# Attention with a transposed score maximum and rescaling on ScalarE, and a convolution over 500 tiles of one bin each, in a graph network kernel

## What is computed

```
feat_all = einsum('ni,rhid->rnhd', inputs, conv_weights)      # 8 relations, 4 heads, 64
el = sum(feat_all[type, src] * attn_l[type], -1)
er = sum(feat_all[type, dst] * attn_r[type], -1)
e  = leaky_relu(el + er, 0.2);  m = segment_max(e, dst)
ex = exp(e - m[dst]);  alpha = ex / segment_sum(ex, dst)[dst]
h  = segment_sum(alpha[..., None] * feat_src, dst) + h_bias
```

```
filt = silu(edge_attr @ Wf1 + bf1) @ Wf2 + bf2                # 20 -> 256 -> 256
agg  = segment_sum(x[dst] * filt, src)
h    = silu(agg @ Wu1 + bu1) @ Wu2 + bu2;  x + batch_norm(h)
```

## Time and profile before

| | us |
|---|---|
| median of 3 runs (lowest, highest) | 4170.91 (4170.29, 4171.05) |
| the profiled execution | 4176.44 |
| its span, first to last instruction | 4174.7 |
| PE busy | 2928.3 |
| DVE busy | 2177.3 |
| ACT busy | 1210.5 |
| POOL busy | 2277.2 |
| mean granted clock of PE | 0.858 of full |

### The profile page before, as it was taken

One profiled execution on the slowest core, in us unless ns is written; L12 is line 12 of the kernel. 1 busy time (PEld: TensorE's weight loads), 2 busy tenths in 40 slices (PEclk: granted clock), 3 DMA queues, 4 the chain that ended last, 5 costly groups with the idle time before them and its releaser, 6 DMA issues. The chain is left out here.

```text
span 4174.7 us, 73619 instructions
## 1 busy us (share of the span) xinstructions
PE 2928.3 (70%) x20296; PEld 2364.7 (57%) x20297; DVE 2177.3 (52%) x5961; ACT 1210.5 (29%) x3266; POOL 2277.2 (55%) x2336
## 2 busy tenths in 40 slices
PE   5199101777777777776379679999999864299990
PEld 1188101555555555555255358888888633288990
DVE  8411002877777777777743557777777444011112
ACT  1123000444444444444223223333333231022220
POOL 2777775777777777777240056666666200511115
PEclk8599655998998999999679789999999875599995
DMA  3344101222222222225100143333335501155533
GB/s 105 108 135 137 40 2 32 63 65 63 63 64 63 64 64 63 64 64 62 23 19 1 47 136 89 90 89 90 90 90 84 52 0 39 49 175 173 171 104 114
DMA packets 209214, 317.71 MB, mean 76 GB/s; under 512 B 63367, under 2 KB 150063, under 8 KB 208388
## 3 DMA queue, kind: packets, MB, share of 16 engines
q0 software_dynamic: 95008, 179.89, 19.9%
q1 hardware_dynamic: 103204, 127.24, 9.4%
q10 hardware_dynamic: 10944, 9.97, 0.7%
HBM read 248.03 MB, written 68.84 MB: 76 GB/s over the span
## 5 line engine op out<-in xcount | busy, mean ns | idle before, releaser
L1402 POOL DMA_INDIRECT conv_got<-xtab,conv_rowidx x588 | 565.8, 962 | 313.2 <-DVE conv_msg L1507 156.6
L806 POOL DMA_INDIRECT att_got<-feat,att_rowidx x588 | 573.2, 975 | 201.5 <-issue 150.2
L294 POOL DMA_INDIRECT table<-l0a_rec,l0a_addr x469 | 458.2, 977 | 216.7 <-issue 146.1
L1454 PE MATMUL conv_pf<-conv_wf,conv_act 128*128 128x256 f32 x2352 | 534.0, 380 | 0.2 <-DVE conv_filt L1502 0.2
L812 POOL DMA_INDIRECT table<-recs_rec,recs_addr x432 | 423.2, 980 | 131.6 <-issue 130.4
L1454 PEld LDWEIGHTS conv_pf<-conv_wf,conv_act 128*128 128x128 f32 x2352 | 447.6, 190 | 76.9 <-issue 0.8
L982 PE MATMUL att_pmax<-all_identb,att_away 128*128 128x512 bf16 x588 | 261.1, 444 | 203.9 <-DVE att_elo L901 203.2
L863 DVE TENSOR_REDUCE att_tmax<-att_pmax 128x4 f32<-128x512 f32 x588 | 373.8, 680 | 31.1 <-PE att_pmax L986 27.6
L986 PE MATMUL att_pmax<-all_identb,att_ehi 128*128 128x128 bf16 x2352 | 383.6, 242 | 0.0
L986 PE MATMUL att_pmax<-all_identb,att_elo 128*128 128x128 bf16 x2352 | 383.3, 242 | 0.0
L1420 ACT ACTIVATE conv_act<-conv_p,conv_bf 128x512 f32<-128x512 f32 x294 | 186.2, 684 | 552.1 <-PE conv_p L1446 552.1
(11 more groups left out here) (336 smaller groups left out, 5074.0 us busy)
## 6 DMA issues: line engine op xcount, KB each, us to landing
moe_w<-in_L_ffn_w SPq DMA_DIRECT2D x96, 512.0 KB
feat<-proj_out SPq DMA_DIRECT2D x30, 1040.0 KB
results<-moe_y ACTq DMA_DIRECT2D x76, 128.0 KB, 1.7
att_got<-feat,att_rowidx POOLq DMA_INDIRECT x588
conv_got<-xtab,conv_rowidx POOLq DMA_INDIRECT x588, 2.8
xtab<-ln_row SPq DMA_DIRECT2D x60, 128.0 KB, 1.7
table<-l0a_rec,l0a_addr POOLq DMA_INDIRECT x469
table<-recs_rec,recs_addr POOLq DMA_INDIRECT x469, 2.1
```

The source lines that it names most:

```text
L294: self.nc.gpsimd.indirect_dma_start(out=self.table, out_offset=bass.IndirectOffsetOnAxis(ap=self.addrs[:, j:j + 1], axis=0), in_=self.recs ...
L806: nc.gpsimd.indirect_dma_start(out=got[g % 3][:, k, :], out_offset=None, in_=feat, in_offset=bass.IndirectOffsetOnAxis(ap=rowidx[:, g * K ...
L1402: nc.gpsimd.indirect_dma_start(out=got[g % 3][:, k, :], out_offset=None, in_=xtab, in_offset=bass.IndirectOffsetOnAxis(ap=rowidx[:, g * K ...
L1454: ins = nc.tensor.matmul(pf[b][:, k, :], act1[s3][:, h, (2 * b + k) * P:(2 * b + k + 1) * P], wf2[:, h, :], start=(h == 0), stop=(h == 1))
```

## The change

In the attention: (1) the pipeline gets a fifth step, with four buffers instead of three for most tiles; the products and sums of a group move from step 2 to step 3, the addition into `acc` from step 3 to step 4. (2) The two bf16 parts of the 16 scores are written into a 128 x 4 x 32 tile `spread` that is otherwise zero; PE turns it (four transposes), ACT copies the result to SBUF (`eT`, 32 x 512), and each tile's maxima matrix is one 512-column matmul for `away` and one 512-column matmul with 32 rows for the scores, in place of 1 + 8 matmuls. (3) The four maxima become one `tensor_reduce` over four PSUM banks, 2048 elements. (4) `acc * keep` is done by ACT, four instructions into `shrunk`; DVE adds the sums with one 260-wide instruction. (5) The type masks are built once for all tiles ahead of the loop. (6) DVE's and ACT's orders in a step are new; bin numbers are read right behind long operations. (7) POOL sends 214 columns of table1 here instead of 432; the rest goes beside the join (12), layer norm 1 (26), the first routing (24), the first mixture (167 instead of 37) and layer norm 2 (26).

In the convolution: table1 has 500 tiles, each of one bin (the ranking pads a bin to 128 edges, not to 512), so 125 groups of 4 tiles whose bins may differ; the sums of the four tiles stay apart, two to a PSUM bank, and DVE makes four additions per group, each with its own bin. The three PSUM banks of the sums are now used two per group.

The diff, cut to its core:

```diff
-ET = 588 (both tables)
+ET1 = 500 (table1)
-COLS1 = ROUND * (ET // K - 3), EJ - ROUND * (ET // K - 3)
+COLS1 = ET // K - 4 + (ET // K - 4) // 2, 12, 26, 24, 167, 26
...
@@ attend, gpsimd
-                if g >= SLOTS:
-                    pool.wait_ge(f_ready, g - 2)
-                    pool.wait_ge(last_ready, (g - 2) * LAST)
+                if g >= SLOTS:
+                    pool.wait_ge(f_ready, g - SLOTS + 1)
+                    pool.wait_ge(last_ready, (g - SLOTS + 1) * LAST)
...
-                for i in range(max(g - SLOTS, 0) * ROUND, max(g - SLOTS + 1, 0) * ROUND):
+            sends = [0 if g < SLOTS else 1 + g % 2 for g in range(GROUPS)]
+                for i in range(sum(sends[:g]), sum(sends[:g + 1])):
...
@@ attend, vector, one step, new order
+                if 0 in parts:
+                    wait_positive(dve, sum_ready, t - 3)
+                    wait_positive(dve, away_ready, t - 3)
+                    v.tensor_tensor(oh[u] ...).then_inc(oh_ready, 1)
+                if 2 in parts:
+                    bin2 = bin_of(dve, t - 2)
+                if 3 in parts:
+                    dve.wait_ge(ex_ready, g + 1)
+                    wait_positive(dve, sum_ready, g - 1)
+                    v.tensor_tensor(f[(u - 3) % 2] ...).then_inc(f_ready, 1)
+                if 4 in parts:
+                    bin4 = bin_of(dve, t - 4)
+                if 1 in parts:
+                    (er picked, reduced, z, e, the two parts into spread).then_inc(e_ready, 1)
+                if 2 in parts:
+                    dve.wait_ge(max_ready, g + 1)
+                    v.tensor_reduce(tmax[:, :], pmax[:, :, :, :].rearrange("p k h e -> p h k e"), AX.XY, ALU.max)
+                    (mnew, drop, mparts[0], m, mparts[1], each waits for the one it reads)
+                if 4 in parts:
+                    dve.wait_ge(sum_ready, g + 1)
+                    dve.wait_ge(shrunk_ready, (g + 1) * HEADS)
+                    v.tensor_tensor(acc at bin4, shrunk, psum[:, 0:HEADS * H1], ALU.add).then_inc(acc_done, 1)
+                if 2 in parts:
+                    dve.wait_ge(me_ready, g + 1)
+                    v.tensor_tensor(below ...).then_inc(below_ready, 1)
...
@@ attend, scalar, one step, new order
+                3: ex, the column of f;  0: away;  3: products(2)
+                4: bin4 = bin_of(act, t - 4)
+                0: ohT (waits turned);  1: eT (waits spread_turned)
+                3: products(3)
+                4: wait_positive(act, acc_done, g); act.wait_ge(keep_ready, g + 1)
+                   for h: nc.scalar.activation(shrunk[:, h, :], acc at bin4, ACT.Copy, scale=keep[s4][:, h:h + 1])
+                2: keep
...
@@ attend, tensor, one step, new order
+                0: transposes of away (waits away_ready)
+                1: transposes of spread (waits e_ready)
+                0: er terms (waits ohT_ready)
+                if 3 in parts:
+                    wait_positive(pe, acc_done, g)
+                    pe.wait_ge(col_ready, g + 1)
+                    pe.wait_ge(f_ready, g + 1)
+                    sums(g, range(ON_DVE + 1))
+                2: pme (waits m_ready)
+                3: sums(t - 3, range(ON_DVE + 1, K)).then_inc(sum_ready, 1)
+                1: for k: matmul(pmax[:, k], away ...); matmul(pmax[:, k], select[:, k:k + 1].broadcast_to([ROWS, P]), eT ...)
...
@@ convolve, tensor
-                    wait_positive(pe, agg_done, t - 6)
-                    for k in range(K):
-                        ... matmul(psum[s4][:, 0:D], oh[s4][:, k, :], msg[s4][:, k, :], start=(k == 0), stop=(k == K - 1))
-                    ins.then_inc(summed, 1)
+                    for b in two:
+                        wait_positive(pe, agg_done, (t - 4) * K + 2 * b - 4)
+                        pe.wait_ge(msg_ready, (t - 4) * 2 + b + 1)
+                        bank = psum[((u - 4) * 2 + b) % 3]
+                        for k in two:
+                            ins = matmul(bank[:, k * D:(k + 1) * D], oh[s4][:, 2 * b + k, :], msg[s4][:, 2 * b + k, :], start=True, stop=True)
+                        ins.then_inc(summed, 1)
...
@@ convolve, vector, end of the step, behind both halves of msg
-                    dve.wait_ge(summed, t - 4)
-                    v.tensor_tensor(at, at, psum[s5][:, 0:D], ALU.add).then_inc(agg_done, 1)
+                    for k in range(K):
+                        n = (t - 5) * K + k
+                        if k % 2 == 0:
+                            dve.wait_ge(summed, (t - 5) * 2 + k // 2 + 1)
+                        wait_positive(dve, agg_done, n)
+                        v.tensor_tensor(at, at, psum[((u - 5) * 2 + k // 2) % 3][:, (k % 2) * D:(k % 2 + 1) * D], ALU.add).then_inc(agg_done, 1)
...
+                join_attention(nc, a, acc, x_res, side1(1))
+                layer_norm(nc, "ln1", c, x_res, xnT, side=side1(2))
+                mixture(nc, c, a, xnT, x_res, side1(3), side1(4))
+                layer_norm(nc, "ln2", c, x_res, xnT, xtab, add=True, side=side1(5))
```

More of the change, by code:

```diff
@@ L735, in attend @@
     LAST = (K - ON_DVE) * HEADS
-    N_DV = (1, 5, K + 4, HEADS - 1)
-    three = range(SLOTS)
+    ROWS = 2 * K * HEADS
+    four = range(SLOTS)
     with Stage(nc, "att") as s:
@@ L786, in in_steps, with bin_of @@
                 peeled(t)
-            with eng.Fori(2, GROUPS // 3) as i:
-                for u in three:
-                    step(i * 3 + u, i, u, {0, 1, 2, 3})
-            for t in range(GROUPS, GROUPS + 3):
+            with eng.Fori(2, GROUPS // SLOTS) as i:
+                for u in four:
+                    step(i * SLOTS + u, i, u, set(range(DEPTH + 1)))
+            for t in range(GROUPS // SLOTS * SLOTS, GROUPS + DEPTH):
                 peeled(t)
+        def bin_of(eng, g):
+            return eng.value_load(bins0[0:1, bass.ds(g, 1)], min_val=0, max_val=NT - 1)
@@ L845, in shrink @@
[L845 to L853 removed]
+                s1, s2, s3, s4 = ((u - d) % SLOTS for d in (1, 2, 3, 4))
@@ new lines, in step @@
+                if 1 in parts:
+                    g = t - 1
+                    act.wait_ge(spread_turned, g + 1)
+                    wait_positive(act, max_ready, g - 1)
+                    nc.scalar.activation(flat(eT[(u - 1) % 2][:, :, :]), pE[:, 0:HEADS * P], ACT.Copy).then_inc(eT_ready, 1)
+                if 3 in parts:
+                    for k in range(ON_DVE + 1, K):
+                        products(k)
+                if 4 in parts:
+                    g = t - 4
+                    wait_positive(act, acc_done, g)
+                    act.wait_ge(keep_ready, g + 1)
+                    for h in range(HEADS):
+                        nc.scalar.activation(shrunk[:, h, :], flat(acc[:, bass.ds(bin4, 1), h, :]), ACT.Copy,
+                                             scale=keep[s4][:, h:h + 1]).then_inc(shrunk_ready, 1)
@@ L1377, in in_steps @@
                     step(i * 3 + u, i, u, {0, 1, 2, 3, 4, 5})
-            for t in range(GROUPS, GROUPS + 5):
+            for t in range(GROUPS // 3 * 3, GROUPS + 5):
                 peeled(t)
```

374 lines of the change are left out of this document (180 added, 194 removed).

## The result

The changed kernel takes **5044.9 us** (median of 4 runs, 5043.5 to 5045.8) where the kernel before takes 4171.0 on the same chip: a ratio of 1.209, 95% interval [1.207, 1.211]. Its profiled execution has a span of 5043.0. The forecast was 4687 with a range of 4300 to 4760: the direction was right, the size wrong by 358 us.

The account below looks back on a forecast made before the run. It took POOL to bound the old attention and PE the convolution. Attention +194, masks and drain +12, convolution +291 and sends +19 gave 516; 4176.4 + 516 - 5.5 = 4687, range 4300 to 4760.

Parts of the forecast that it names:

- The chains: Waits of PE for DVE's additions set the step at full clock: attention 8.85 us, convolution 8.0 us.
- The bin reads I cost at nothing: DVE's bin number reads in the loops priced at zero; without cover each costs up to 0.33 us.
- I take 1.4, once a group: Attention: a clock fall behind PE's 2.5 us gap costs 1.4 us per group, making the step 10.25 us.
- My upper end, 1.7: Both loops: a 3.4 us stretch at half clock costs at most 1.7 us per group.
- Two falls in three groups, 1.15: Convolution: clock falls of 1.7 us in two of three groups add 1.15, to 9.15 to 9.2 a step.
- Moved sends: Sends moved out of the attention cost 19 us in the mixture.
- Elsewhere nothing, and if the cover fails 2 us each: Sends outside the mixture cost nothing; layer norm 1, the tightest, covers 33 us of sends within 36.7.
- Sum: Whole kernel: 194 + 12 + 291 + 19 = 516 us more, to 4687.
- The long maximum: Attention, DVE: one maximum over 2048 elements takes 2.29 us where four took 2.48, worth 0.19.
- Rival 1: Both loops: the clock mostly holds, full-clock steps give 160 us more, 4331; chance 0.18.
- Rival 3: Attention: faster, the loop follows POOL at 7.0 us a step, total 4060, or 3790; chance 0.12.

Follow-up runs that it names:

- d4: c3 with the four bin reads of a convolution step moved to its beginning: 5324.5 us, on a chip where the kernel before takes 5272.9.
- c3: The changed kernel with two more, unread matmuls of 512 columns in each convolution step, between the two halves of the sums: 4856.4 us.
- c4: The changed kernel with four more, unread matmuls of 256 columns in each attention step, behind the er terms: 4723.6 us.
- e4: The changed kernel with sends back in the attention (three per group), the last 40 in the mixture, none beside join, layer norms and routing: 5004.1 us.
- e2: The kernel before with only its sends moved as in the change: 3962.4 us, ratio 0.950.
- d2: The same kernel as e2 on another chip: 5026.8 us for 5272.9, ratio 0.953.
- g2: The changed kernel, DVE's acc addition ahead of its maximum, ACT rescaling a group earlier, convolution's first two additions ahead of bias additions, reads spread: 4956.4 us, ratio 0.937.

## Why the prediction was wrong in size, point by point

- **The chains.** Right in kind: the two waits stand where the prediction put them (2.5 and 2.4 us; I had 2.5 and 2.0 to 2.2), the one-hot matrix waits for the sums, POOL for the products. In size the attention is 9.50 at full clock for 8.85, 96 us over 147 steps, and the convolution 8.47 for 8.04, 54 us over 125.
- **"The bin reads I cost at nothing."** This step failed: 0.36 of the convolution's 0.43 are reads, by the rows of d4 beside c3; a step shorter by as much was not seen. I had seen the row that bounds one of them, and then took the end at which it is covered; the convolution of the change has four a step on DVE. In the attention the reads' share of the 0.65 was not separated.
- **"I take 1.4, once a group."** The step that failed most. The clock costs 11.83 - 9.50 = 2.33 us a step of the attention, 137 us more than I had. I had reckoned with one stretch of 3.4 us at half clock per group and 0.9 of slack in the maxima. But it mostly stays low for 17 us of 23.9, and then the eight matmuls of the maxima, 0.54 apart instead of 0.32, use the slack up and hold the next maximum by 0.76 in the step shown. The sums and pme cost more, too: from the end of the addition to the one-hot matrix are 4.65 us in the step shown of the changed kernel, at the lower level, and 2.56 in that of c4, 2.1 between them. My upper end, 1.7, was no bound: it was a price of one fall, taken from a loop that recovered between falls.
- **"Two falls in three groups, 1.15."** The convolution's clock costs 10.02 - 8.47 = 1.55 a step, 49 us more: it falls in all but four of 116 steps.
- **Moved sends.** From routing to layer norm 2, where the mixture lies, they cost 24 us for the forecast 19. "Elsewhere nothing, and if the cover fails 2 us each" held for layer norm 1, which is 0.4 us longer than before (though e4, without sends there, takes 7 less), and failed for the join: layer norm 1 starts 12.8 us later, since three sends take 8 us each instead of 1. I had checked the count of sends against the length of layer norm 1, and not what DVE does in the join ahead of it.
- **Sum.** 516 forecast, about 870 measured: 96 + 54 more in the chains, 137 + 49 in the clock, 19 between the stages.
- **The long maximum.** 2.29 us for four of 2.48, as worked out. A full drain between the four, as the Trainium skill ("VectorE: DVE Perf Modes", Terms) has it, would have made the gain 0.43 a step; but the four already took 2.48 and not 4 x 0.68, so here the measurement decides.
- **Rival 1, the clock holds.** Wrong: filling the gaps took off 321 and 188 us (c4, c3), 6.4% and 3.7% of the 5045. This is far over the figure of the Trainium skill that was weighed for it ("TensorE: Matmul & The Clock Gate", Part 1, a ramp penalty of under 1% of a typical span). In a loop with a gap in every step the penalty is paid in nearly every step, and I should not have weighed a figure for a whole span there; the measurement decides.
- **Rival 3, POOL rules.** Its place and its price were right for the old loop: 7.23 by e2, for the 7.0 of 5.5 DMAs. The new loop never came near it.
- Range: its upper end was made of my prices at their bounds, so a mechanism priced by the wrong kind of row put the result outside.

## What to carry to other kernels

If a change gives a loop a wait of PE that comes in every step, price the clock as a state of the loop and not as single falls: work the step out once with all of PE's operations at half clock, and see whether what had slack still has it. Here the steps at the lower level throughout took 12.75 and those at the upper 9.50, and the mean came to 11.83, nearer the lower clock. Before an operation is cut into tiles that save work on one engine, count the operations and the reads of index numbers that it adds on the engine beside it (125 steps for 147 here, but 7.12 us for 5.84). And try each part of a change by itself: here one of its parts was worth 5% in the kernel before, hidden in a change that costs 21%.

## What the runs showed of the hardware that was not expected

- **Sends beside long DVE operations.** The three 7680-element operations of the join, which read two tensors in SBUF, take 8.16 us each, and three sends that POOL issues beside them took 8.30, 7.89 and 7.88 for the usual 0.96, each ending 0.8 us behind the end of DVE's operation; where DVE was not in such an operation they took 0.96 again. The Trainium skill has this: by "SBUF — State Buffer", the part on the two separate sides, DVE and GpSimd share a pair of ports as an exclusive lock, held for a whole instruction, also where DVE's has two inputs in SBUF and GpSimd's reads SBUF. The trace agrees.
- **Reads of an index number.** A read into a register costs DVE 0.16 to 0.2 us behind a 0.69 operation (c3), and where four stand together they follow at 0.71 us each (d4).
- **Chips.** The same kernel before takes 4169 to 4174 us on one and 5235 to 5289 on three others. The ratio of the moved sends carried over (0.950 in e2, 0.953 in d2), others did not: the changed kernel with c3's filler is at 1.165 (c3), and with the reads moved as well at 1.010 on the other kind (d4). g2 is 6% faster than the kernel before there, and was not tried on the first kind. What makes the three slower was not found.
